# A two-layer graph network on one core: more tiles fetched row by row from byte addresses, and the first gathers put ahead of a branch

## What is computed

```python
h = relu(layernorm(x))
m = (h @ W.T + b)[src] * edge_weight[:, None]
x = x + segment_sum(m, dst)                       # layer 0
h = relu(layernorm(x))
for t in range(4):                                # layer 1, 4 edge types
    m_t = relu(concat(h[src], h[dst]) @ W1[t] + b1[t]) @ W2[t] + b2[t]
agg = segment_sum(m_t of each edge's own type, dst)
x = x + GRU(agg, h)                               # sigmoid, sigmoid, tanh gates
```

## Time and profile of the kernel before

| | us |
|---|---|
| median of 3 runs (lowest, highest) | 2103.95 (2102.8, 2105.99) |
| the profiled execution's own time | 2105.3 |
| its span, first to last instruction | 2103.3 |
| POOL busy in the span | 1552.7 (74%) |
| PE busy | 1257.6 (60%) |
| DVE busy | 900.4 (43%) |
| ACT busy | 572.3 (27%) |

### The profile page before, as it was taken

One profiled execution on the slowest core, in us unless ns is written; L12 is line 12 of the kernel. 1 busy time (PEld: TensorE's weight loads), 2 busy tenths in 40 slices (PEclk: granted clock), 3 DMA queues, 4 the chain that ended last, 5 costly groups with the idle time before them and its releaser, 6 DMA issues.

```text
span 2103.3 us, 35010 instructions
## 1 busy us (share of the span) xinstructions
PE 1257.6 (60%) x6646; PEld 1073.7 (51%) x6646; DVE 900.4 (43%) x2549; ACT 572.3 (27%) x1502; POOL 1552.7 (74%) x1644
## 2 busy tenths in 40 slices
PE   2545545545545545445556767777766777667776
PEld 2433433433333333333345666666666666666665
DVE  7732332332232332333234555555555555555554
ACT  4633333333333333333231111111111111111111
POOL 6777777777777777777567777777777777777774
PEclk7565666666666667666578888888889888998887
DMA  8333323323333333333244444444444444444442
GB/s 192 95 79 83 99 79 91 92 79 94 89 81 92 89 79 93 89 81 92 71 130 113 107 112 115 119 111 112 121 111 114 118 113 109 120 114 113 119 114 60
DMA packets 182878, 214.76 MB, mean 102 GB/s; under 512 B 56894, under 2 KB 128973, under 8 KB 182156
## 3 DMA queue, kind: packets, MB, share of 16 engines
q0 software_dynamic: 52192, 106.99, 21.0%
q1 hardware_dynamic: 125608, 103.77, 17.1%
q10 hardware_dynamic: 4856, 1.72, 0.4%
HBM read 176.32 MB, written 35.99 MB: 101 GB/s over the span
## 4 chain that ended last, share of the span: by engine, by line
POOL 71%; issue 23%; PE 2%; DMA 1%; DVE 1%; ACT 1%; ACTq 0%; POOLq 0%; SPq 0%; DVEq 0%
POOL accs L1338 35%; POOL G L1698 15%; POOL edge L1698 15%; POOL g_more L1698 7%; PE bank L1625 1%; DMA accs<-h_tab,src_t 1%; PE bank L1588 1%; DMA accs<-in_edge_weight_dram 0%; ACT accs L1500 0%; ACTq L440 0%; PE bank L1894 0%; DMA p_tab<-hot 0%; DMA edge<-p_tab,src_t 0%; PE bank L1603 0%; ACTq L425 0%
## 5 line engine op out<-in xcount | busy, mean ns | idle before, releaser
L1338 POOL DMA_INDIRECT accs<-h_tab,src_t x758 | 716.1, 945 | 231.2 <-issue 230.0
L1883 PE MATMUL bank<-qwin,hotT 128*128 128x128 f32 x1662 | 294.0, 332 | 305.3 <-DVE hotT L1766 294.1
L1588 PE MATMUL bank<-accs 128*125 128x133 f32 x1662 | 327.1, 367 | 213.0 <-ACT accs L1500 164.9
L1588 PEld LDWEIGHTS bank<-accs 128*125 128x125 f32 x1662 | 305.8, 270 | 256.3 <-issue 146.1
L1883 PEld LDWEIGHTS bank<-qwin,hotT 128*128 128x128 f32 x1662 | 250.3, 231 | 340.3 <-DVE hotT L1766 326.8
L1698 POOL DMA_INDIRECT G<-p_tab,src_t x331 | 313.6, 947 | 121.8 <-issue 100.7
L1698 POOL DMA_INDIRECT edge<-p_tab,src_t x328 | 311.0, 948 | 100.0 <-issue 100.0
L1500 ACT ACTIVATE accs<-accs,edge 128x128 f32<-128x128 f32 x758 | 243.1, 390 | 467.2 <-DMA accs<-h_tab,src_t 374.2
L1836 ACT ACTIVATE rows<-rows 128x512 f32<-128x512 f32 x208 | 130.9, 629 | 625.5 <-DVE rows L1776 576.1
L1894 PE MATMUL bank<-hot,rows 128*128 128x128 f32 x1662 | 281.6, 326 | 2.3 <-ACT rows L1836 1.5
L1894 PEld LDWEIGHTS bank<-hot,rows 128*128 128x128 f32 x1662 | 264.7, 242 | 3.0 <-ACT rows L1836 2.8
(11 more groups left out here) (178 smaller groups left out, 1332.3 us busy)
## 6 DMA issues: line engine op xcount, KB each, us to landing
qwin<-q_tab SPq DMA_DIRECT2D x416, 64.0 KB
hotT<-h_tab SPq DMA_DIRECT2D x1162, 0.5 KB
hotT<-h_tab ACTq DMA_DIRECT2D x896, 0.5 KB
w1a<-p_tab ACTq DMA_DIRECT2D x896, 0.5 KB
nodew<-key_tab SPq DMA_DIRECT2D x52, 256.0 KB
nodehot<-key_tab SPq DMA_DIRECT2D x52, 256.0 KB
w1a<-p_tab SPq DMA_DIRECT2D x778, 0.5 KB
accs<-h_tab,src_t POOLq DMA_INDIRECT x758
```

The lines of the kernel that those rows point to most:

```text
L1338: eng.indirect_dma_start(slot0(o % R0)[:, t, 0:D], None, x if o < EARLY else h0_tab, bass.IndirectOffsetOnAxis(src_t[:, k:k + 1], 0)).then ...
L1588: ins = eng.matmul(pb[SUM_BANK[o % 4]][0:CW, 0:FW], ones_of(o % HR)[:, t, :], slot0(o % R0)[:, t, :], start=t == 0, stop=t == last)
L1883: ins = eng.matmul(pb[2 + g % 2][:, t * D:(t + 1) * D], hotT[:, g % HT, t * P:(t + 1) * P], qwin[:, g % NG, t // PR, :], start=True, stop= ...
```

## The change

It has three parts. The row numbers are stored as byte places, already times 512, in two tables (layer 0 had used `src` itself), and each row DMA addresses a byte view of the table with a register's value as it is. The tiles by rows rise from 9 to 13 (SP) and from 7 to 9 (ACT) in layer 0, and from 6 to 9 and from 7 to 12 in layer 1, each tile's rows spread over fewer steps. `src` is loaded ahead of `dst`, and POOL issues the first octet's gathers ahead of `choose`.

```diff
+    place_tab0 = nc.dram_tensor("place_tab0", [NT * P], I32).ap()
+    place_tab1 = nc.dram_tensor("place_tab1", [NT * P], I32).ap()
+    h0_bytes = h0_tab.rearrange("n d -> (n d)").bitcast(U8)
+    p_bytes = p_tab.rearrange("n d -> (n d)").bitcast(U8)
...
+        ROW = 4 * D
...
-        rows_sp0 = ByRow("sp", [spread((18 + 10 * j) * TO + TO - 1, 6 + 10 * j, 10) for j in range(9)] + [TAIL0],
+        rows_sp0 = ByRow("sp", [spread((15 + 7 * j) * TO + TO - 1, 6 + 7 * j, 7) for j in range(13)] + [TAIL0],
...
-        rows_sp1 = ByRow("sp", [spread((36 + 32 * j) * GT + GT - 1, 2 + 32 * j, 32) for j in range(6)] + [TAIL1],
+        rows_sp1 = ByRow("sp", [spread((27 + 22 * j) * GT + GT - 1, 2 + 22 * j, 22) for j in range(9)] + [TAIL1],
...
-        rows_act0 = ByRow("act", [spread((22 + 13 * j) * TO + TO - 2, 14 + 26 * j, 26) for j in range(7)],
+        rows_act0 = ByRow("act", [spread((19 + 10 * j) * TO + TO - 2, 14 + 20 * j, 20) for j in range(9)],
...
-        rows_act1 = ByRow("act", [spread((30 + 26 * j) * GT + GT - 1, 2 + 26 * j, 26) for j in range(7)],
+        rows_act1 = ByRow("act", [spread((20 + 16 * j) * GT + GT - 1, 2 + 16 * j, 16) for j in range(12)],
...
         def sp_prologue(eng):
-            load_edges(eng, dst, dst_i, 1, "dst_in")
-            load_edges(eng, src, src_i, 2, "src_in")
+            load_edges(eng, src, src_i, 1, "src_in")
+            load_edges(eng, dst, dst_i, 2, "dst_in")
...
         def sp_row_numbers(eng):
-            eng.wait_ge(s["row_no"], 1)
-            eng.dma_start(row_tab.rearrange("(p e) -> p e", p=PB), typ_i.rearrange("p g e -> p (g e)")).then_inc(s["row_st"], 16)
+            for k, (tab, a) in enumerate(((place_tab0, src_i), (place_tab1, typ_i))):
+                eng.wait_ge(s["row_no"], k + 1)
+                eng.dma_start(tab.rearrange("(p e) -> p e", p=PB), a.rearrange("p g e -> p (g e)")).then_inc(s["row_st"], 16)
...
-                    rows.held[:] = row_values(eng, rows, j, r, N - 1)
-                eng.dma_start(rows.rows_of(j)[r:r + 1, :], h0_tab[bass.ds(rows.held[r % BATCH], 1), :]).then_inc(rows.sem[j % 2], 16)
+                    rows.held[:] = row_values(eng, rows, j, r, (N - 1) * ROW)
+                eng.dma_start(row_bytes(rows, j, r), h0_bytes[bass.ds(rows.held[r % BATCH], ROW)].rearrange("(a d) -> a d", a=1)).then_inc(rows.sem[j % 2], 16)
...
         def act_row_numbers(eng):
+            eng.activation(src_i, src_a, ACT.Copy, scale=float(ROW)).then_inc(s["row_no"], 1)
             eng.wait_ge(s["keys_in"], 1)
-            eng.activation(typ_i, src4_a, ACT.Copy).then_inc(s["row_no"], 1)
+            eng.activation(typ_i, src4_a, ACT.Copy, scale=float(ROW)).then_inc(s["row_no"], 1)
...
+        def pool_first_octet(eng):
+            eng.wait_ge(s["preC"], 1)
+            octet_rows(eng, 0, x)
+
         def f0_pool(eng):
-            eng.wait_ge(s["preC"], 1)
-            for o in range(NOCT):
+            for o in range(1, NOCT):
...
-            row_numbers(eng, rows_act0, 0, src)
...
             for o in range(-WEIGHED0, STEPS0):
+                if o == EARLY - 1:
+                    eng.wait_ge(s["row_st"], 32)
+                    row_numbers(eng, rows_act0, 0, place_tab0)
...
-            row_numbers(eng, rows_sp0, 0, src)
+            eng.wait_ge(s["row_st"], 32)
+            row_numbers(eng, rows_sp0, 0, place_tab0)
...
         @block.gpsimd
         def _(eng):
             pool_prologue(eng)
             pool_sums(eng)
+            pool_first_octet(eng)
             choose(eng, [f0_pool, f1_pool], [pool_h0, l0_pool, l1_pool])
```

More of the change, by code:

```diff
@@ L27 @@
 I32 = mybir.dt.int32
+U8 = mybir.dt.uint8
 ACT = mybir.ActivationFunctionType
@@ L241, in gnn_program @@
                           for who in ((rows_sp0, rows_act0), (rows_sp1, rows_act1)))
-        assert NTILE == NT - 1 and NTILE % GT == 3 and len({k // GT for k in alone1}) == len(alone1) == 14 and len(alone0) == 17
+        assert NTILE == NT - 1 and NTILE % GT == 3 and len({k // GT for k in alone1}) == len(alone1) == 22 and len(alone0) == 23
         def gathered0(o, h):
@@ L426, in row_values, with row_bytes @@
                 rows.numbers[0:1, a:b], engines=[eng.engine], min_val=0, max_val=top,
-                skip_runtime_bounds_check_because="they are row numbers of the graph's edges, as the gathers read them")
+                skip_runtime_bounds_check_because="they are places of rows of the graph's edges, which the gathers read too")
             return v
+        def row_bytes(rows, j, r):
+            return rows.rows_of(j)[r:r + 1, :].bitcast(U8)
         def rows0(eng, rows, step):
@@ L433, in rows0 @@
                 eng.wait_ge(rows.known, 16 * (rows.loads + j + 1))
-                row_numbers(eng, rows, j + 1, src)
+                row_numbers(eng, rows, j + 1, place_tab0)
                 if j >= 2:
@@ L445, in rows1 @@
                 eng.wait_ge(rows.known, 16 * (rows.loads + j + 1))
-                row_numbers(eng, rows, j + 1, row_tab)
+                row_numbers(eng, rows, j + 1, place_tab1)
                 if j >= 2:
@@ L450, in rows1 @@
                 if r % BATCH == 0:
-                    rows.held[:] = row_values(eng, rows, j, r, N * T - 1)
-                eng.dma_start(rows.rows_of(j)[r:r + 1, :], p_rows[bass.ds(rows.held[r % BATCH], 1), :]).then_inc(rows.sem[j % 2], 16)
+                    rows.held[:] = row_values(eng, rows, j, r, (N * T - 1) * ROW)
+                eng.dma_start(row_bytes(rows, j, r), p_bytes[bass.ds(rows.held[r % BATCH], ROW)].rearrange("(a d) -> a d", a=1)).then_inc(rows.sem[j % 2], 16)
         def sp_x(eng):
+            for h in range(2):
+                eng.wait_ge(s_g0[0][h], 16 * GT)
             for i, (a, b) in enumerate(PIECES):
@@ L616, in dve_pads @@
         def dve_pads(eng):
+            eng.memset(src_i[LR:PB, :, :], 0).then_inc(s["pads"], 1)
             eng.memset(dst_i[LR:PB, :, :], int(FAR)).then_inc(s["pads"], 1)
-            eng.memset(src_i[LR:PB, :, :], 0).then_inc(s["pads"], 1)
             eng.memset(typ_i[LR:PB, :, :], 0).then_inc(s["pads"], 1)
@@ L886, in sweep_end @@
                 apart(eng)
-                for k in (q[0] for q in s_g0[:NG]):
+                for k in (q[0] for q in s_g0[1:NG + 1]):
                     eng.dma_reset(range(k.num, k.num + 1))
@@ L1010, in step @@
                 eng.wait_ge(*grp("hot0", g))
-                eng.wait_ge(s_g0[g.slot][0], g.gathered)
+                eng.wait_ge(s_g0[g.slot + 1][0], g.gathered)
                 pairs_in(eng, "acc0", g, back=1)
@@ L1325, in pair_at, with octet_rows @@
             return c if r == 0 and 0 <= c < NPAIR else None
+        def octet_rows(eng, o, table):
+            for t in range(TO):
+                k = o * TO + t
+                if k in alone0 or k >= NTILE:
+                    continue
+                eng.indirect_dma_start(slot0(o % R0)[:, t, 0:D], None, table,
+                                       bass.IndirectOffsetOnAxis(src_t[:, k:k + 1], 0)).then_inc(s_g0[o % R0][t // GT], 16)
+        def pool_first_octet(eng):
+            eng.wait_ge(s["preC"], 1)
+            octet_rows(eng, 0, x)
         def f0_pool(eng):
-            eng.wait_ge(s["preC"], 1)
-            for o in range(NOCT):
+            for o in range(1, NOCT):
                 if o >= R0:
@@ L1333, in f0_pool @@
                     eng.wait_ge(s["tab"], 32 * len(T_PIECES))
-                for t in range(TO):
-                    k = o * TO + t
-                    if k in alone0 or k >= NTILE:
-                        continue
-                    eng.indirect_dma_start(slot0(o % R0)[:, t, 0:D], None, x if o < EARLY else h0_tab,
-                                           bass.IndirectOffsetOnAxis(src_t[:, k:k + 1], 0)).then_inc(s_g0[o % R0][t // GT], 16)
+                octet_rows(eng, o, x if o < EARLY else h0_tab)
         def f0_dve(eng):
@@ L1735, in finished @@
                 eng.dma_start(out[c * CW:(c + 1) * CW, :], o_st[0:CW, :]).then_inc(s["upd_st"], 16)
-            eng.wait_ge(s["row_st"], 16)
-            row_numbers(eng, rows_sp1, 0, row_tab)
+            eng.wait_ge(s["row_st"], 32)
+            row_numbers(eng, rows_sp1, 0, place_tab1)
             for g in range(-2, STEPS1):
@@ L1857, in f1_act @@
             eng.wait_ge(s["c_q"], NPAIR)
-            eng.wait_ge(s["row_st"], 16)
+            eng.wait_ge(s["row_st"], 32)
             eng.wait_ge(s["st_p"], PQ_STORED)
-            row_numbers(eng, rows_act1, 0, row_tab)
+            row_numbers(eng, rows_act1, 0, place_tab1)
             for g in range(-1, STEPS1):
```

4 lines of the change are left out of this document (1 added, 3 removed).

## The result

| | before | after |
|---|---|---|
| median, runs of both kernels side by side, us | 2104.97 (4 runs, 2102.8 to 2107.03) | 2078.99 (4 runs, 2077.72 to 2081.74) |
| the profiled execution's own time, us | 2105.3 | 2078.96 |
| its span, us | 2103.3 | 2077.2 |

The ratio is 0.9878, interval 0.9861 to 0.9896: 26 us less, with 21.9 to 29.3 us in the interval. The gain of 1.2% is small, but its interval is clear of none. The forecast was 2081.05 us, 22.9 less, in a range of 2077.5 to 2087.5.

The account below looks back on a forecast made before the run. POOL's gathers, issued one behind the other, were taken as the bound. Fewer gathers (17.5 us) plus the start (5.4) made 22.9, so 2103.95 - 22.9 = 2081.05 us, range 2077.5 to 2087.5.

Parts of the forecast that it names:

- The bound: Both layers: POOL issues gathers back to back, held by nobody; each tile taken from it saves its pitch, about 1.25 us.
- Fewer gathers, 17.5 us: POOL loses 6 gathers in layer 0 and 8 in layer 1, 14 x 1.25 = 17.5 us.
- Price of a row, 0.339 us: SP's row DMAs: arithmetic goes with its gap, the MOVE stays; a row falls from 0.413 to 0.339 us.
- SP's time in layer 0: SP's queue owes 34.4 of 38.8 us per four octets and so keeps up, still waiting some 110 us for ACT.
- Even the upper bound costs about nothing: Layer 0: at 0.413 us a row SP falls 24 us short over the layer, and the ring swallows 40.
- the ring: Buffer of six octets, 48 tiles, between POOL's gathers and PE's sums; some 40 us of room in layer 0.
- the arithmetic does not go: Rival, chance 0.08: rows stay at 0.413 us; 2081, or 2085 to 2095 if SP's late stores stretch the layer turn.
- The start, 5.4 us: `src` first and gathers ahead of the branch start octet 1 4.7 to 6.5 us earlier; 5.4 taken.
- The lock between DVE and POOL: Early gathers: two 0.75 us DVE passes could lock POOL out and take up to 1.5 us of the head start.
- Octet 7: POOL enters octet 7 at 85.0 us, after `h0_tab` is stored at 78.2 to 81.7: no wait, 3 to 7 us room.
- Turn and end: The turn between the layers and the stretch behind POOL's last gather stay as long as before.
- slower: Rival, chance 0.04: SP's queue becomes the bound in layer 0 at over 0.435 us a row; 2217 us at 0.50.

Follow-up runs that it names:

- the run with nearly no rows: Changed kernel with two whole tiles by rows in place of 43, so 41 more gathers; quiet condition: 2132.85 us, ratio 1.014 to the kernel before.
- the old arithmetic: Changed kernel with rows addressed by row number again, register multiplication back; ratios to the kernel before: quiet 2090.68 us, 0.9924; stalling 3168.42 us, 1.109.
- the changed kernel's second trace: Changed kernel run again unaltered in the third set, beside the kernel before, quiet condition: 2082.56 us, ratio 0.9893.
- the old start: Changed kernel with `dst` loaded before `src` and all gathers behind the branch again; stalling condition: 2895.35 us, ratio 1.0127 to the kernel before.
- old tiles: Changed kernel with the kernel before's 29 tiles by rows in place of 43; ratios to the kernel before: quiet 2101.61 us, 0.9972; stalling 2635.32 us, 0.9224.

## Why the prediction was right

The time (2078.99) lies 2.1 us below the forecast; against the kernel before beside it the gain is 26.0 us, 3.1 more than the 22.9 forecast. The mechanism is the one that it gave. That the sum came so close is in part luck: in the first pair of traces the fewer gathers brought less than forecast, the start more, and the end 3.5 us that were in no step. By its steps:

- **The bound.** Right. Two edits of the number of gathers alone gave 49.4 us for 41 and 19.3 (by ratios 16.6) for 14, 1.2 to 1.4 us each. "A tile is worth its whole pitch" holds within that over a range from 2 to 43 tiles by rows, with byte places and in the quiet condition.
- **Fewer gathers, 17.5 us.** The first pair of traces gave 14.7 in the two layers, the sets since then 16.6 by ratios and 19.3 by spans (17.9 in the layers). The forecast lies among them. In the first pair the pitch of layer 1 is 1.256 us in place of 1.253, which took 2.3 us back; why is open, as the run with nearly no rows has 1.257 too.
- **Price of a row, 0.339 us.** Measured 0.327; the MOVE stayed, as assumed, and 12 ns more of gap went with the arithmetic.
- **SP's time in layer 0.** The model said a wait for ACT of about 110 us left; it was 166.2. The cheaper row explains 25 x 73.1 x 0.012 = 22 us of the 56. The rest is more than covered by a count: the model has rows in all 25 pairs of chunks, 1828 in all, but they are spread over 91 of the 104 octets, and the trace has 1674; 154 rows fewer are 50 us at 0.327.
- **"Even the upper bound costs about nothing."** Wrong, and the step whose mechanism failed; the result did not rest on it, as the row was cheaper. At 0.413 us a row the old arithmetic costs 8.8 us. The step counted the ring of 48 tiles, which covers POOL, and not the end of the layer: the last whole tile by rows belongs to octet 99, ACT waited 12.4 us for its rows, and only four octets come after it, too few to make that good. Its shortage, 24 us over the layer, was too small as well: the last row left 42.5 us later than in the changed kernel. The rival "the arithmetic does not go" had the turn as the place, though by late stores and not by late rows, and said 2085 to 2095; the median measured was 2090.68. So taking the arithmetic out was no side matter: it carries 6.5 us by the ratios (0.9924 - 0.9893; some 2 to 11 by the intervals) and 8.8 by the spans, and with it left in, 14 more tiles bring 10.9 us (2101.61 to 2090.68) in place of 17 to 19.
- **The start, 5.4 us.** By ratio 5.9 (3.8 to 8.0); by the first pair of traces 7.4 at the 57th gather, by the changed kernel's second trace 90.48 - 84.57 = 5.9. In the first pair the parts were off and made up for each other. `src_t` was there sooner (first gather at 11.58 us, not 12.7), the branch cost nothing instead of 1.4 us, and the gather of 1.97 us that seemed part of the first eight moved behind them, where it takes its 1.03 us a little later: 8.50 us won at the ninth gather, 7.40 kept. In the other four quiet traces the ninth came at 22.84 to 23.84 us and 5.6 to 6.6 us were kept.
- **The lock between DVE and POOL.** The Trainium skill ("SBUF — State Buffer", Who interferes with whom) has a DVE instruction in a two-port mode and a GpSimd instruction shut each other out of the shared ports: the one issued first holds them for the whole instruction. From that the forecast had two 0.75 us passes cost up to 1.5 us. The trace of the result agrees only in part: the gather that begins 0.02 us behind the start of the first pass (19.45 us) takes 0.95, none too long, and the one beside the end of the second takes 1.08, 0.14 too long. In the second trace of the changed kernel the gather beside both takes 1.30, 0.36 too long. What cost more there was not one of these two: the next gather took 1.66, and it begins 0.38 us into the pass of line 689, which reads two f32 inputs, when the 0.75 us passes have ended. The kernel before has that too (1.52 us at 20.22, beside line 677), and the forecast passed over it. The gather before, and the one in the second trace of the changed kernel:

```profile
20.22 1.52 POOL L1338 DMA_INDIRECT accs<-in_x_dram,src_t  x1 [0.30 <-issue]
...
21.59 1.66 POOL L1344 DMA_INDIRECT accs<-in_x_dram,src_t  x1 [0.30 <-issue]
```

- **Octet 7.** Right: no wait, 32 tiles summed where 16 were needed.
- **Turn and end, "as long as they were".** The turn yes (21.51, 22.01, against 22.03). The end was 3.5 us shorter in the first pair, with the granted clock of PE at 1.00 in place of 0.50; whether that was chance or comes with the other tiles is open.
- **The rival "slower" (0.04).** It didn't happen in the result, but it is what happens in the stalling condition, by a mechanism that no row of before shows: stalls of 0.7 us on the queues that issue the rows, SP's above all. The rule of the Trainium skill ("DMA: Bandwidth & Descriptors", Rules for kernel authors) against small transfers was set aside in the forecast by rows of the quiet condition. In the quiet condition the rule fails (43 tiles as 512-byte pieces beat 2 by 50 us). In the stalling condition fewer pieces were faster, as the rule has it (29 tiles took 2635 us, 43 at the old start 2895), though by the stalls at issue; two tiles were not run there.

Still open is the cause of the stalls. They hit MOVE and DMA records alike on SP and ACT, and the gaps between them. A MOVE is no transfer, so slow transfers alone would not explain it. PE was not spared either: its weight loads of line 1904 stood 388.7 us there in waits for nothing that the profile shows (old tiles). Whether it is how the instructions reach the queue, or what they leave behind, no run tells.

## What to carry to other kernels

When a tile is handed from the bounding engine to a queue with slack, the profit is its whole pitch; to see whether the queue keeps up, look at its remaining wait per period *and* at what stands behind it where the stage ends, for a ring hides lateness inside a stage and not at its end: the last piece handed over should be due well before the stage closes. A table of ready-made byte places saves the register arithmetic in front of each piece, here 0.09 of 0.41 us, and that can decide how many pieces pay. Judge two parts of a start together: loading first and gathering first gave -1.1 and +2.5 us alone and 7.5 together.

## What the hardware showed that was not expected

- The same kernel took 2104 us and 2857 us on the same chip at different times, without any change in POOL's own operations (line 1344's mean gather is 0.945 us in the result and 0.946 in a stalling run). What the profile shows in its place is about a thousand records on SP's queue of 0.7 us each and nearly as many gaps of that length between them. A kernel that issues thousands of small DMAs should be timed in more than one session: the order of versions turned round (old tiles with byte places: 0.3% faster than before in the quiet condition, 7.8% in the stalling one; 43 tiles with arithmetic: 0.8% faster, 10.9% slower).
- POOL reads a flag and takes a branch while its gather is under way: the gap before the ninth is 0.31 us, like the others.
- One DVE pass of 1.22 us made the gather that begins 0.06 us behind it 1.03 us longer in every trace; on ACT it does not.
- The granted clock behind the last gather was 0.50 in one trace and 1.00 in another for nearly the same work, and the end was 3.5 us longer in the first.
